# Two places in turn for the decays of a state-space scan: a PSUM bank and a row block in SBUF

## The reference, cut to what matters

```
A = -jnp.exp(A_log)
def step(state, xs):
    d_t, B_t, C_t, u_t = xs
    dA = jnp.exp(d_t[..., None] * A)
    state = state * dA + (d_t * u_t)[..., None] * B_t[:, None, :]
    y_t = jnp.einsum('ben,bn->be', state, C_t)
    return (state, y_t)
...
x = x + jnp.tanh(g_xattn[0]) * _L0_xattn_ref(ctx_1024, _layernorm(x), ...)
x = x + jnp.tanh(g_ffn[0]) * _L0_ffn_ref(_layernorm(x), ...)
```

## Time and profile before

| what | value |
|---|---|
| median of 3 runs | 1927.52 us |
| the profiled execution's own time | 1928.64 us |
| its span in the trace | 1926.8 us |
| PE, DVE, ACT, POOL busy | 1553.0, 1179.3, 887.9, 809.6 us |
| the 192 scans of rounds 0 to 2 | 234.4 us, 1221 ns each |
| the stretches in which they run | 278 to 465, 547 to 735, 816 to 1000 us |

### The profile page before, as it was taken

How to read it: one execution, slowest core, us unless ns; L and a number is a source line. 1 busy time by engine, 2 the same in 40 slices (tenths; PEclk the granted TensorE clock), 3 DMA queues, 4 the chain that set the end, 5 groups by cost and what they waited for, 6 DMA issues and landing times.

```text
span 1926.8 us, 26809 instructions
## 1 busy us (share of the span) xinstructions
PE 1553.0 (81%) x9216; PEld 1185.3 (62%) x9216; DVE 1179.3 (61%) x1730; ACT 887.9 (46%) x1973; POOL 809.6 (42%) x809
## 2 busy tenths in 40 slices
PE   5246877777967778777769787899999999999995
PEld 2234544555645555545547455778788899999973
DVE  4689658887578886589863343333332566656545
ACT  4443446664356663566641573121211466666510
POOL 0595135552256541366532121144321455655544
PEclk8555986888967898968888997999999999999997
DMA  5620001210101110001101112722120577777464
GB/s 196 234 77 22 23 6 33 61 45 28 40 22 50 50 39 29 11 28 55 45 23 66 56 40 80 314 83 93 50 71 1 197 251 252 250 249 261 153 236 158
DMA packets 92374, 191.56 MB, mean 99 GB/s; under 512 B 8704, under 2 KB 25600, under 8 KB 88912
## 3 DMA queue, kind: packets, MB, share of 16 engines
q1 hardware_dynamic: 87120, 173.07, 26.0%
q0 software_dynamic: 5120, 16.78, 2.6%
HBM read 136.21 MB, written 53.61 MB: 99 GB/s over the span
## 4 chain that ended last, share of the span: by engine, by line
PE 42%; DVE 5%; issue 5%; ACT 3%; POOL 3%; DMA 0%; DVEq 0%; ACTq 0%; SPq 0%; POOLq 0%
PE scores L528 21%; PE bank L528 12%; POOL yab L1947 2%; PE scores L647 1%; PE bank L675 1%; PE bank L592 1%; DVE YA L1396 1%; ACT EX L1051 1%; PE bank L839 1%; PE bank L660 1%; DVE HS L1386 1%; PE bank L702 1%; ACT PT L1059 1%; DVE nm L1438 1%; ACT bank L1016 1%
## 5 line engine op out<-in xcount | busy, mean ns | idle before, releaser
L1796 POOL TENSOR_TENSOR GB<-DU,BB 128x512 f32<-128x512 f32 x256 | 326.8, 1289 | 127.1 <-DVE HS L1386 68.1
L592 PE MATMUL bank<-ident,HS 128*128 128x128 f32 x896 | 185.3, 343 | 173.0 <-DVE YA L1396 118.6
L1386 DVE TENSOR_TENSOR_SCAN HS<-bank,GB 128x512 f32<-128x512 f32 x224 | 273.7, 1222 | 48.4 <-ACT bank L1016 23.9
L592 PEld LDWEIGHTS bank<-ident,HS 128*128 128x128 f32 x896 | 125.1, 172 | 222.7 <-DVE YA L1396 157.8
L1016 ACT ACTIVATE bank<-DL,aneg 128x512 f32<-128x512 f32 x224 | 154.9, 692 | 132.1 <-DVE HS L1386 130.8
L1396 DVE SCALAR_TENSOR_TENSOR YA<-bank,Ct,YA 128x512 f32<-128x512 f32 x224 | 165.0, 737 | 28.4 <-PE bank L592 26.3
L1059 ACT ACTIVATE PT<-bank 128x128 f32<-128x128 f32 (+3 forms) x256 | 110.8, 433 | 113.8 <-PE bank L660 112.5
L528 PE MATMUL scores<-xth,wgh 128*128 128x256 f32 x552 | 158.1, 286 | 2.1 <-DVE fa L1682 1.2
L528 PE MATMUL scores<-xth,wgl 128*128 128x256 f32 x552 | 156.1, 283 | 0.0
L528 PE MATMUL scores<-xtl,wgh 128*128 128x256 f32 x552 | 156.1, 283 | 0.0
L660 PE MATMUL bank<-ident,EX 128*128 128x128 f32 x640 | 129.5, 303 | 24.6 <-ACT PT L1059 23.3
(11 more groups left out here) (245 smaller groups left out, 3849.0 us busy)
## 6 DMA issues: line engine op xcount, KB each, us to landing
wgr<-wffn_in SPq DMA_DIRECT2D x108, 384.0 KB, 6.3
wdr<-wffn_in SPq DMA_DIRECT2D x81, 256.0 KB, 3.4
BB<-b_scratch SPq DMA_DIRECT2D x64, 256.0 KB, 3.2
xg<-V SPq DMA_DIRECT2D x1, 11776.0 KB, 38.8
xr<-xg SPq DMA_DIRECT2D x23, 512.0 KB, 5.7
yg<-ysb SPq DMA_DIRECT2D x23, 512.0 KB, 6.2
hah<-hhd SPq DMA_DIRECT2D x5, 1024.0 KB, 5.9
hal<-hhd SPq DMA_DIRECT2D x5, 1024.0 KB, 8.0
```

What stands on the lines that cost most here:

```text
L592: mm = nc.tensor.transpose(state_bank(s, q)[:, et * P:(et + 1) * P], HS[:, n % 2, et, tt * P:(tt + 1) * P], ident[:])
L1386: nc.vector.tensor_tensor_scan(HS[:, n % 2, et, :], decay_bank(s, k), GB[:, k % 4, :], 0.0, ALU.mult, ALU.add).then_inc(scan_done, 1)
L1796: nc.gpsimd.tensor_tensor(GB[:, k % 4, :], DU[:, et, :], BB[:, n % 2, :], ALU.mult).then_inc(gb_ready, 1)
```

## The change

In rounds 0 to 2 odd blocks' decays go to a new SBUF block `decays` (128x512 f32), declared and released just before `xd`, so it covers the same addresses, and even blocks' decays stay in HT1. A decay now waits for the scan before the last and not for the last one. Three waits go with the shared place. Decay 1 of a sequence waits until B is stored and C is turned. `xdbl`, which writes xd, waits until the scans of the sequence before are done. Decay 0 no longer names a scan. Round -1 keeps its two banks.

```diff
+        sd = ExitStack()
+        DB = arena(sd)("decays", [P, L])
+        sd.close()
         xd = mid("xd", [N3, L])
...
         def decay_bank(s, k):
-            return (HT1, A[1])[k % 2] if s == 0 else HT1
+            return (HT1, A[1] if s == 0 else DB[:])[k % 2]
...
             def xdbl(s):
                 act.wait_ge(xd_mm, s + 1)
                 at(act, b_stored, 16 * s)
+                at(act, scan_done, NB * s)
...
-                if k > (s == 0):
-                    act.wait_ge(scan_done, NB * s + k - (s == 0))
+                if k == 1:
+                    act.wait_ge(b_stored, 16 * (s + 1))
+                    act.wait_ge(ct_mm, s + 1)
+                if k > 1:
+                    act.wait_ge(scan_done, NB * s + k - 1)
```

## The result

The changed kernel takes 1937.69 us (median of 10 runs, 1932.50 to 1942.22), the kernel before in the same sessions 1930.22 us (10 runs, 1926.19 to 1933.23). The ratio is 1.0040, with a 95% interval of 1.0026 to 1.0054: slower by 7.5 us. The forecast said no change, 1927; the interval of the ratio leaves no change out, and the side is that of rival C. The profiled execution took 1939.83 us.

A forecast was written before the change was run, and what follows sets the result against it. DVE was taken to bound the kernel, beside a PE turning loop of equal length where PE is slow. Half the gains and half the losses, -18.5 + 17.8 us, gave 1927 us, no change; range 1912 to 1943.

The forecast's parts named there:

- rival C: Tied POOL products start first, each step's second scan stands a whole product: 12.8 us on the path, 1940; chance 0.27.
- DVE first, two loops beside each other: Rounds 0 to 2: DVE busiest, decay loop equals PE's turning loop at 1.2 GHz; slack 37 us, stepped gain 15.6.
- The first step: Each round's first step, where decay waits are worst: 1.3 us shorter without blocking, 0.7 us kept with it.
- The write and the read alone: Odd decay's write to SBUF 0.73 us, hidden behind a scan; odd scan's SBUF read 1228 ns, 0.5 us in all.
- The read beside POOL: Odd scans with two SBUF inputs stand until POOL's product ends, less 0.14 us at 72 scans: 35.6 us.
- The sum: Gains 37 and losses 35.6 us in the same places on DVE; half of each: -18.5 + 17.8, or -0.7 us.
- The step through one step: Step 7 of round 1, followed scan by scan: odd steps on middle widths lose 0.5 us and more.
- Rivals A and B: A: blocking misses the scan, 1912, chance 0.18. B: PE's turning loop and row maximum hold all, 1923.5, chance 0.10.
- The three new waits: Waits before decay 1 and xdbl are met long before and hold nothing queued behind them: 0 us.

The follow-up runs named there:

- without POOL: POOL's products cut to 8 of 512 columns: in the changed kernel 1901.52 us (ratio 0.9852), in the kernel before 1923.02 us (0.9966).
- the price without the gain: Changed kernel with its two decay places, but each decay again waiting for the last scan: 1949.76 us, ratio 1.0102 to the kernel before.
- the moved product: POOL's product 4q+4 issued before the context remainder: on the changed kernel 1926.53 us (ratio 0.9988), on the kernel before 1928.42 us (0.9994).
- the two half kernels: Changed kernel with SBUF decays only for each step's second block: 1936.46 us (ratio 1.0034); only for its fourth block: 1926.35 us (0.9984).

## Why the prediction was wrong

- *DVE first, two loops beside each other.* Right as far as it goes: decay waits were worth something, 21.5 us without POOL. I had stepped it to 15.6 and bounded it by 37, so 58% of the slack came back as time, what the clock adds in step 4 included.
- *The first step.* 0.7 us expected with blocking, 1.4 measured; 1.3 expected without it, 2.3 measured with POOL short (6.37 against 8.67). Undersized.
- *The write and the read alone.* Right: 0.716 for 0.73, and 1.232 without POOL for 1.228.
- *The read beside POOL.* Right in kind: a held scan ends mostly 1.07 to 1.10 after POOL's instruction, for 1.07. The total, 35.1 us for 35.6, is right partly by luck, since the places moved: the second scans of step 8, where a product had 1.09 us left in the kernel before, are not held in any round, and those of step 9, with 0.57 left, stand still 0.96.
- *The sum.* This is the step that failed. It puts gain and price at half each and adds them, -18.5 + 17.8, as if neither changed the other. Each one alone came out near that: the gain is 21.5 us of 37 (58%), the price without the gain 20.3 us of 32.1 (63%), and -21.5 + 20.3 would again be no change. Together they don't add: the kernel is 7.5 us slower, because the gain beside the price is worth 12.1 us, or the price beside the gain 29 us, 83% of the 35.1. This interaction of 9 us the sum put at nothing. The likely reason is that waits for PE took up 16 us of the price where the decays still waited and none where they no longer did, so the two drew on the same slack. That the losses come in pieces of about 1 us at the second scan, in front of the additions that PE's turning waits for, and the gains in pieces of 0.2 to 0.3, fits it, but no run separates this from the granted clock, which is lower in round 0 of the changed kernel (0.73 for 0.78).
- *The step through one step.* Step 7 was to lose 0.5 to 0.7. It lost 0.15 in round 1, 0.2 in round 2 and 2.4 in round 0, where its second scan took 2.15. In rounds 1 and 2 it was POOL that stood still at the second scan (three products took 4.76 us together from 623.59 on, for 3 x 1.28). Of the 2.4 in round 0, 0.9 is its second scan; the step ran at a clock of 0.64 for 0.82. The sum had no term for the clock.
- *Rival C.* Its mechanism is what happened in steps 2 and 3 of rounds 1 and 2, and its place, the second scan, is where most of the loss comes in, as the moved product and the two half kernels say. Its time, 1940, is nearer than the forecast's, but its condition did not hold: 15 of 48 second scans took over 2 us, not all, and the whole standing still is 35.1 us, not the 61 (35.6 + 3 x 8.5) that it supposes. That its price of 12.8 us comes near the 7.5 is therefore luck. Rivals A and B fell: the blocking reaches the scan, and the decay slack did not come back as waits for PE.
- *The three new waits.* Nothing stands behind them in the waits view, but no run tried them alone.

## What to carry to other kernels

Before a PSUM operand of VectorE moves to SBUF, count the operation's other SBUF inputs, and look in the trace at what GpSimd does at each of its starts. The remainder there was a good estimate of how long it stood still in total, but not of the places, since these move, nor of what it cost: weigh each piece against the slack at its own place. A shorter hold-up in one place (22.7 us at second scans, 1936 us) can cost more than a longer one in another (51.4 us at first and third scans, 1927 us). Nor do a gain and a price on one engine simply add, as both may draw on the same waits. And compare the granted clock of each step before a difference of a us or two in it is put down to the change. Where the blocking can't be avoided, moving GpSimd's instruction past a small one, or keeping the old place in some steps, can turn a loss into a gain.

## What the runs showed of the hardware that I had not expected

- When both start at almost the same time, either can stand still, and the recorded order mostly tells which: the scan at 571.12 behind a product from 571.11, and in the kernel with the moved product the GpSimd operation at 562.99 behind a scan from 562.98 (1.46 us instead of 0.46). But not always. In step 3 of round 0 of the changed kernel the product is recorded first, by 0.02 us, and it is the product that stands still:

```profile
308.77 1.21 DVE L1393 TENSOR_TENSOR_SCAN HS<-decays,GB 128x512 f32<-128x512 f32 x1
308.75 2.29 POOL L1803 TENSOR_TENSOR GB<-DU,BB 128x512 f32<-128x512 f32 x1
```

- The scan overlaps some of its start with the hold-up: it ends 1.07 to 1.09 us after the product in the blocks shown, though it takes 1.21 alone.
